# The low parts of delta and delta*x: made by GpSimd in every chunk, by VectorE in none

## The reference

```
xz = xn @ in_proj_w.T;  x, z = split(xz)            # 256 inner channels each
x = silu(causal depthwise conv of 4 taps over x)
dt_r, B, C = per-head projection of x               # 4 heads of 64 channels, 16 states
delta = softplus(per-head projection of dt_r + dt_b)
for every token t:                                  # state s: 256 channels x 16 states
    s = s * exp(delta_t * A) + (delta_t * x_t) * B_t
    y_t = sum over the 16 states of s * C_t
y = (y + x * Dskip) * silu(z);  out1 = y @ out_proj_w.T
out2 = mixture of experts: softmax gate, top 1 of 8 experts with capacity 1024,
       relu(tokens @ W1 + b1) @ W2 + b2, times the gate
result = input + out1 + out2
```

## Time and profile before

| | |
|---|---|
| median of 3 runs | 1313.71 us (1312.18 to 1315.65) |
| the profiled execution | 1312.99 us, span of the trace 1311.1 us |
| VectorE busy | 1113.3 us, 85% of the span |
| TensorE busy (matmuls) | 1052.0 us, 80% |
| GpSimd busy | 864.6 us, 66% |
| ScalarE busy | 803.8 us, 61% |
| mean granted TensorE clock | 0.902 of full speed |

### The profile page before, as it was taken

How to read it: one execution, slowest core, us unless ns; L and a number is a source line. 1 busy time by engine, 2 the same in 40 slices (tenths; PEclk the granted TensorE clock), 3 DMA queues, 4 the chain that set the end, 5 groups by cost and what they waited for, 6 DMA issues and landing times.

```text
span 1311.1 us, 15848 instructions
## 1 busy us (share of the span) xinstructions
PE 1052.0 (80%) x3949; PEld 523.5 (40%) x3949; DVE 1113.3 (85%) x1364; ACT 803.8 (61%) x1245; POOL 864.6 (66%) x708
## 2 busy tenths in 40 slices
PE   0766568889889989889899988887888878788775
PEld 0432234545444454545445453343333333343322
DVE  7658879797887979798896979999998989999996
ACT  3574357676676866666675766656575666656521
POOL 2327887575665757576575758677776868686755
PEclk9987779999999999999999999879887979878766
DMA  6512122121113121120212112111212121210211
GB/s 148 151 45 66 44 86 66 40 73 40 47 26 80 32 71 42 40 72 7 74 32 80 32 40 57 27 42 29 57 40 52 44 49 48 48 48 0 61 43 42
DMA packets 62905, 69.62 MB, mean 53 GB/s; under 512 B 11488, under 2 KB 49280, under 8 KB 62848
## 3 DMA queue, kind: packets, MB, share of 16 engines
q1 hardware_dynamic: 58752, 60.65, 18.6%
q0 software_dynamic: 4096, 8.40, 2.1%
HBM read 18.69 MB, written 16.78 MB: 27 GB/s over the span
## 4 chain that ended last, share of the span: by engine, by line
POOL 37%; issue 29%; PE 18%; DVE 6%; SPq 3%; DMA 3%; ACT 3%; POOLq 1%; DVEq 0%; ACTq 0%
POOL s_sb L565 24%; POOL expert_in L572 4%; POOL xn L543 4%; POOL dd L523 3%; DMA dsp<-dd 3%; DVE u_sb L909 2%; PE bank L1126 2%; PE bank L1225 2%; DVE s_sb L982 2%; PE bank L1192 2%; POOL dd L533 2%; PE bank L1185 2%; PE bank L1203 2%; PE bank L1210 2%; SPq L396 1%
## 5 line engine op out<-in xcount | busy, mean ns | idle before, releaser
L565 POOL TENSOR_TENSOR s_sb<-s_sb,c_of 128x512 f32<-128x512 f32 x480 | 628.6, 1312 | 344.9 <-DVE s_sb L982 339.1
L982 DVE TENSOR_TENSOR_SCAN s_sb<-bank,u_sb 128x512 f32<-128x512 f32 x512 | 619.1, 1209 | 0.0
L760 ACT ACTIVATE bank<-bank,a_neg 128x510 f32<-128x510 f32 x512 | 336.5, 661 | 260.5 <-PE bank L1210 244.9
L909 DVE TENSOR_TENSOR u_sb<-bank,b_of 128x512 f32<-128x512 f32 x512 | 345.5, 675 | 143.0 <-PE bank L1203 132.1
L1203 PE MATMUL bank<-dsp,sel_d 128*128 128x512 f32 x512 | 329.2, 643 | 47.3 <-DMA dsp<-dd 23.2
L1210 PE MATMUL bank<-dsp,sel_d 128*128 128x512 f32 x512 | 241.2, 471 | 71.6 <-DVE s_sb L982 68.4
L1203 PEld LDWEIGHTS bank<-dsp,sel_d 128*128 128x128 f32 x512 | 107.0, 209 | 198.2 <-DVE u_sb L909 111.0
L1210 PEld LDWEIGHTS bank<-dsp,sel_d 128*128 128x128 f32 x512 | 107.5, 210 | 193.8 <-DVE s_sb L982 152.8
L1225 PE MATMUL bank<-s_sb,con 128*32 128x512 f32 x1024 | 152.8, 672 | 13.2 <-POOL s_sb L565 9.3
L1126 PE MATMUL bank<-xnT,wx 128*128 (+1 forms) x256 | 129.7, 601 | 0.0
L1159 PE MATMUL bank<-bc,sel_bc 128*128 128x512 f32 x128 | 60.2, 522 | 43.5 <-ACT b_of L721 26.4
(11 more groups left out here) (146 smaller groups left out, 1225.3 us busy)
## 6 DMA issues: line engine op xcount, KB each, us to landing
dsp<-hi SPq DMA_DIRECT2D x64, 256.0 KB
dsp<-dd SPq DMA_DIRECT2D x64, 256.0 KB
expert_in<-dd SPq DMA_DIRECT2D x8, 512.0 KB, 6.5
xn<-expert_in SPq DMA_DIRECT2D x8, 512.0 KB, 4.3
xn<-L_ffn_W SPq DMA_DIRECT2D x16, 256.0 KB, 4.5
expert_out<-xn SPq DMA_DIRECT2D x16, 256.0 KB, 2.5
out<-acc SPq DMA_DIRECT2D x8, 512.0 KB, 5.2
expert_in<-xn,put_at POOLq DMA_INDIRECT x64
```

Of the source, the lines that this page charges most:

```text
L565: pool.tensor_tensor(s_now, s_now, c_of[:, hf, hh, :], ALU.mult).then_inc(S["p_ready"], 1)
L760: act.activation(d, d, ACT.Exp, scale=a_neg[:, k:k + 1]).then_inc(S["decay_ready"], 1)
L909: dve.tensor_tensor(u_sb[:, w % U_RING, :], du_ps[w % 2][:, :], b_of[:, hf, head_of(w), :], ALU.mult).then_inc(S["u_ready"], 1)
L982: dve.tensor_tensor_scan(s_sb[:, w % S_RING, :], decay_of(w)[:, :], u_sb[:, w % U_RING, :], 0.0, ALU.mult, ALU.add).then_inc(S["scan_done" ...
```

## The change

The function `low_by_pool` goes, VectorE's `split_low` goes with its call, and GpSimd's call of its own `split_low` stands without the condition. Operands, sizes, semaphores and all else stay.

```diff
-        def low_by_pool(ch):
-
-            return has_ffn(ch)
...
                     for of, hf_, _ in softplus_now(ch, w, "scale"):
                         scale_x(of, hf_)
-                    if low_by_pool(ch):
-                        for of, hf_, _ in due("low"):
-                            split_low(of, hf_)
+                    for of, hf_, _ in due("low"):
+                        split_low(of, hf_)
...
-            def split_low(ch, hf):
-
-                dve.wait_ge(S["hi_ready"], per_chunk(ch, 2, hf + 1))
-                dve.tensor_tensor(lo, dd, hi.bitcast(F32), ALU.subtract).then_inc(S["lo_ready"], 1)
...
-                    if not low_by_pool(ch):
-                        for of, hf_, _ in softplus_now(ch, w, "low"):
-                            split_low(of, hf_)
```

## The result

The changed kernel takes 1337.32 us, median of 4 runs (1333.33 to 1338.93), beside 1314.08 us before (4 runs): ratio 1.0173, 95% interval 1.0146 to 1.02, so +23.2 us against the +15.2 forecast. That is above the forecast's own range (1322 to 1336 us) and at the upper edge of the stated one (1317 to 1337). The medians, ratios and intervals of this document leave out two executions in a second, slower state, 1569.52 us of i_hi_first_before and 1387.41 us of l_late_hi_first. The profiled execution after took 1333.33 us (span 1331.5), 20.3 more than the profiled one of before.

What follows compares the result with a forecast made beforehand. GpSimd was taken to bound chunk 0 and VectorE chunks 9 to 14. The terms 11.6 + 5.8 + 0 - 2.2 = +15.2 us gave a median of 1329 us, own range 1322 to 1336, stated range 1317 to 1337.

Steps and rivals of the forecast that it cites:

- Chunk 0, +11.6: Chunk 0: GpSimd's subtractions and the late landing behind them delay VectorE's restart, +11.6 us, bounds +4.7 and +15.
- Chunks 9 to 14, half 0, +1.0 each: Slot 25, six times: VectorE's 1.1 us won is spent waiting for the spread, and 1.0 more: +5.8 us.
- Chunks 9 to 14, half 1, 0 each: Slot 8, six times: VectorE's 2.25 us lead is all given back waiting for slot 16's spread: 0 us.
- TensorE slow to restart: Half 1 of chunks 9 to 14: part of the upper bound of +1.5 us, with gather and product slow as before.
- Chunk 15, -2.2: Half 1 of chunk 15: the u comes at 1257.1 instead of 1259.42, and the kernel's end follows: -2.2 us.
- Heavier in the gather chunks: Chunks 9 to 14: GpSimd falls further behind in slots 8 to 11; 12 us more, 1341 us, chance 0.12.
- The delay is absorbed: Late landing hides behind other lateness: chunk 0 costs 4.7, half 0 nothing, chunk 15 gives 2.2; 1316 us, chance 0.08.
- VectorE's time counts in full: Chunks 9 to 14 get 20.3 us back, if the landing takes under about 4 us; 1303 us, chance 0.06.

Runs made afterwards that it cites:

- i_hi_first_before: Kernel before, with SyncE issuing the two DMAs of hi as soon as hi is there: 1309.94 us, ratio 0.9968.
- l_late_hi_first: Kernel before, with GpSimd subtracting in chunks 1 to 15, VectorE in chunk 0, and the DMAs of hi issued first: 1299.99 us, ratio 0.9895.
- a_first_only: Kernel before, with the subtraction moved to GpSimd in chunk 0 too, VectorE keeping chunks 9 to 15: 1324.26 us, ratio 1.0076.
- c_half0_only: Kernel before, with GpSimd making the low part of half 0 only (slot 25) in chunks 9 to 14: 1319.54 us, ratio 1.0039.
- g_warm: Changed kernel, with 14 and 8 idle TensorE matmuls ahead of the spreads of slots 0 and 16 in chunks 9 to 15: 1323.75 us, ratio 1.0061.
- k_combine_15: Changed kernel, with VectorE's eight combines in slots 15 to 22 instead of 14 to 21 of chunks 9 to 15: 1333.6 us, ratio 1.0148.
- f_pool_early: Kernel before, with GpSimd subtracting in chunks 1 to 15, in chunks 9 to 15 at slots 6 and 23, not 8 and 25: 1303.56 us, ratio 0.9933.
- d_half1_only: Kernel before, with GpSimd making the low part of half 1 only (slot 8) in chunks 9 to 15: 1318.78 us, ratio 1.004.

## Why the prediction was right, and where it was off

- **Chunk 0, +11.6.** Measured +11.4, and alone in a_first_only +11.4. The product of slot 15 was to be 5.05 us late and was 5.0; the landing was 7.4 us where 7.3 was taken.
- **Chunks 9 to 14, half 0, +1.0 each.** Right in size: c_half0_only has +1.0 each, 6.1 us over the stretch. The 2.6 us that the working took for TensorE's restart came from a row at the lower clock (0.50 over the 6 us from 854.61 on in the kernel before), so the clock's price was in the sum here without being named; g_warm shows it.
- **Chunks 9 to 14, half 1, 0 each.** This step failed. In the kernel after, scan 20 stands 0.2 us earlier in chunk 9 and 1.3 to 1.6 us later in each of chunks 10 to 14, 7.1 us in sum; the other 4.4 of the 11.5 are half 0's (in these chunks somewhat less than when alone). The step followed the work to the u of slot 16, forecast equal to before and measured 0.47 us late in chunk 10, and stopped there. The limit stands four slots on: 45 matmuls lie between that spread and scan 20, the last that matters the spread of delta*x for slot 21. They had 14.35 us before; the spread comes 2.0 us later in the chunk, which leaves 12.3, enough at a granted clock of 1.00 (12.13) and not at 0.88 (13.69). "TensorE slow to restart" was in the bound of +1.5 of this step, and the value was taken as 0, though the trace of before has TensorE at 0.50 to 0.56 over the 6 us behind the spreads of slot 0 in chunks 10 to 15, where their own waits were only 0.4 to 0.9 us.
- **Chunk 15, -2.2.** Measured -1.3. The u of slot 16, which answers to the last of the earlier trace rows, does come 2.2 us sooner, at 1278.87, 32.02 from the chunk's start against 34.29. Then the clock takes back 1.0: over the 6 us behind the awaited spread the granted clock is 0.52 (1.00 before), and VectorE waits 0.88 us for the next u. With matmuls in the wait (g_warm) it is 0.94 and the chunk 1.1 us shorter.

```profile
1277.97:1283.97 6.00, 5.79 (x16) 2.36 (x16) 4.45 (x8) 1.98 (x3) 2.59 (x2) 0.52 0.00 0
```

- **The rivals.** "Heavier in the gather chunks" had the place, half 1, and nearly the size, but not the mechanism: the landing starts when the working said, GpSimd's lag does block VectorE's combine, but this alone costs 0.4 us, and adding work to TensorE takes most of the loss of chunks 9 to 14 away (g_warm). "The delay is absorbed" is refuted by the waits. "VectorE's time counts in full" named its condition rightly, a landing of about 4 us: with 4.5 to 4.8, the kernel does get faster, though by two fifths of the freed time in chunks 9 to 14.
- **The sum.** Half 1 was too low by 7.1, chunk 15 by 0.9, half 0 too high by 1.4, chunk 0 by 0.2; these and the first scan, 0.6 sooner, and chunks 1 to 8, 0.6 shorter, give the 20.4 of the profiled executions. With a term of 7.1 us missed, it is luck that the median came to stand at the edge of the stated range and no further. The medians differ by 2.9 more. That remains open: the other runs of the kernel after lie at 1336.75 to 1338.93, its profiled one at 1333.33, and only the profiled one has a trace. A chunk 9 like that of k_combine_15, whose scan 20 is 2.5 us later than in the traced run of after, would make such a difference, but no trace of the kernel after shows it.

## What to carry to other kernels

When a step is moved to an idle engine, look at what its result travels through: here 7.4 us of DMAs stood between the moved instruction and its reader, and how late it reached its reader decided the sign, not either engine's load: with the subtraction two slots earlier (f_pool_early), or with a shorter landing, the same move gains. When an engine is made to wait where it did not, follow it to the next place at which someone needs it, not only to the instruction that waited, and sum its work there at the lower clock too. And let a transfer wait for its own data alone: one reordered loop turned the ratio of the same change from 1.0173 to 0.9936, and with chunk 0 left as it was to 0.9895. The loop gains by itself on the kernel before, though (0.9968); beside that kernel the two are an estimated 0.997 and 0.993.

## What the runs showed of the hardware

- **TensorE's clock behind a wait.** In chunks 10 to 14 of the kernel after, waits of 3.1 to 3.4 us on the spread of slot 16 were followed by a granted clock of 0.72 over the next 6 us, which means part of it at the lower of the two levels, 1.2 GHz; the wait of 2.30 us in chunk 9 was followed by 1.00. The wait's length alone does not say it: d_half1_only has one of 3.26 us followed by 1.00 and one of 1.95 followed by 0.72. With matmuls in the wait it was 1.00 in chunks 9 to 14.
- **VectorE and GpSimd excluding each other.** VectorE's combine of 128x128 took 0.32 us alone and 1.86 to 1.91 (3.00 in d_half1_only) when it met a train of GpSimd products; VectorE's subtraction 1.2 alone and up to 3.90; GpSimd's product 1.27 alone and 2.18 beside that subtraction.
- **Four DMAs or two.** In chunks 9 to 15 of the kernel after, four of 256 KB issued together landed 7.2 to 7.5 us after the end of the subtraction that released them; with two of them sent ahead (l_late_hi_first), it was 4.5 to 5.1 where TensorE waited for it.
